# Selective scan: output gate moved into the weights, residual rows added by TensorE, finished tiles copied by ScalarE

## The reference, cut to what matters

```python
shift, scale, gate = split(silu(c) @ ada_w.T + ada_b)    # gate: one row of 512 for each batch
xn = layernorm(x) * (1 + scale) + shift
x_in, z = split(xn @ in_proj_w.T)                        # 1024 channels each
u = silu(causal_conv4(x_in) + conv_b)
dt_r, B, C = split(u @ x_proj_w.T)                       # 64, 16, 16
dt = softplus(dt_r @ dt_proj_w.T + dt_proj_b)
h = h * exp(dt * A) + (dt * u) * B                       # step by step in time, 16 states for each channel
y = (sum over states of h * C) + u * D_param
out = x + gate * ((y * silu(z)) @ out_proj_w.T)
```

## Time and profile before

| | |
|---|---|
| median of 3 runs | 5542.39 us (5534.5 to 5546.62) |
| the profiled execution | 5539.89 us |
| its span | 5538.1 us |
| first stage, first to last instruction of VectorE | to 2130 us of the span |
| busy over the span | TensorE 90%, VectorE 77%, GpSimd 65%, ScalarE 58% |
| mean granted clock of TensorE | 0.97 |

### The profile page before, as it was taken

One profiled execution on the slowest core, in us unless ns is written; L12 is line 12 of the kernel. 1 busy time (PEld: TensorE's weight loads), 2 busy tenths in 40 slices (PEclk: granted clock), 3 DMA queues, 4 the chain that ended last, 5 costly groups with the idle time before them and its releaser, 6 DMA issues. The chain is left out here.

```text
span 5538.1 us, 62588 instructions
## 1 busy us (share of the span) xinstructions
PE 4962.2 (90%) x20224; PEld 2738.9 (49%) x20224; DVE 4265.5 (77%) x5656; ACT 3193.6 (58%) x5887; POOL 3596.6 (65%) x2406
## 2 busy tenths in 40 slices
PE   7888989898989877988999999999998888988998
PEld 2333333333333324764444444444443677776777
DVE  6999999999999995447777777777774565656565
ACT  3757575766667552225888888888886223232323
POOL 3879797978788773224889888988988322222222
PEclk9999999999999998997999999999999999999999
DMA  4021212211121203331111111111111412111212
GB/s 175 23 107 38 92 51 90 89 53 77 53 81 50 91 16 116 133 132 33 28 32 36 24 36 24 36 34 26 36 24 46 157 57 78 37 69 67 78 37 69
DMA packets 119638, 350.72 MB, mean 63 GB/s; under 512 B 13104, under 2 KB 14352, under 8 KB 104912
## 3 DMA queue, kind: packets, MB, share of 16 engines
q1 hardware_dynamic: 102448, 300.76, 16.8%
q0 software_dynamic: 9216, 33.56, 1.6%
q10 hardware_dynamic: 7648, 12.41, 0.7%
HBM read 278.49 MB, written 67.67 MB: 63 GB/s over the span
## 5 line engine op out<-in xcount | busy, mean ns | idle before, releaser
L431 POOL TENSOR_TENSOR mamba_hc<-mamba_h,mamba_bc 128x1024 f32<-128x1024 f32 x512 | 1217.0, 2377 | 353.6 <-DVE mamba_h L664 299.7
L812 PE MATMUL mamba_y<-mamba_hc,ident 128*128 128x512 f32 x2048 | 1004.7, 614 | 262.9 <-POOL mamba_hc L431 261.8
L1364 POOL TENSOR_TENSOR attn_pair_sum<-attn_pair_sum,attn_prob 128x1024 f32<-128x1024 f32 x512 | 1203.9, 2386 | 54.0 <-ACT attn_prob L1479 54.0
L1523 DVE TENSOR_REDUCE attn_mx<-attn_ps_max 128x1 f32<-128x512 f32 x1536 | 967.7, 685 | 317.2 <-PE attn_ps_max L1387 312.7
L1479 ACT ACTIVATE attn_prob<-attn_ps_s 128x512 f32<-128x512 f32 x2048 | 1051.3, 602 | 76.4 <-PE attn_ps_s L1414 76.4
L534 ACT ACTIVATE mamba_da<-mamba_dt,mamba_a_neg 128x512 f32<-128x512 f32 x1024 | 690.0, 689 | 692.7 <-DVE mamba_h L664 689.4
L664 DVE TENSOR_TENSOR_SCAN mamba_h<-mamba_da,mamba_state,mamba_h 128x512 f32<-128x512 f32 x768 | 940.1, 1266 | 1.9 <-ACT mamba_da L534 1.9
L1414 PE MATMUL attn_ps_s<-attn_q_stack,attn_k_stack 100*128 100x512 f32 x2048 | 884.9, 436 | 5.2 <-ACT attn_prob L1479 5.2
L1387 PE MATMUL attn_ps_max<-attn_k_stack,attn_q_stack 98*128 98x512 f32 x2048 | 833.2, 412 | 37.7 <-DMA attn_q_stack<-qk_parts 19.8
L812 PEld LDWEIGHTS mamba_y<-mamba_hc,ident 128*128 128x128 f32 x2048 | 371.4, 192 | 844.1 <-POOL mamba_hc L431 429.5
L654 DVE TENSOR_TENSOR mamba_h<-mamba_du,mamba_bc 128x1024 f32<-128x1024 f32 x512 | 619.6, 1210 | 65.5 <-POOL mamba_state L433 57.3
(11 more groups left out here) (302 smaller groups left out, 7475.1 us busy)
## 6 DMA issues: line engine op xcount, KB each, us to landing
mamba_bc<-bc_dram SPq DMA_DIRECT2D x64, 1024.0 KB, 7.3
mamba_w<-in_in_proj_w_T SPq DMA_DIRECT2D x16, 2048.0 KB, 7.8
qk_parts<-qkv_pair POOLq DMA_DIRECT2D x64, 512.0 KB, 3.2
attn_k_stack<-qk_parts SPq DMA_DIRECT2D x96, 256.0 KB
attn_q_stack<-qk_parts SPq DMA_DIRECT2D x96, 256.0 KB
mamba_x_in<-in_x SPq DMA_DIRECT2D x16, 1024.0 KB, 5.6
mamba_w<-in_out_proj_w_T SPq DMA_DIRECT2D x8, 2048.0 KB, 8.4
lin_norm_x<-x_after_L SPq DMA_DIRECT2D x16, 1024.0 KB, 5.6
```

What stands on the lines that cost most here:

```text
L431: nc.gpsimd.tensor_tensor(hc[:, gs % HC_SLOTS, :, :], h[:, gs % H_SLOTS, :, :], bc[:, g, G:2 * G, :], ALU.mult).then_inc(s["hc_done"], 1)
L812: mm = nc.tensor.matmul(y[ct % 2][:, :], ident[:, :], hc[:, gs % HC_SLOTS, j, :], start=(g == 0 and j == 0), stop=(g == NG - 1 and j == G ...
L1364: nc.gpsimd.tensor_tensor(pair_sum[(hd * NGRP + g) % 2][:, at], first[:, at], prob[unit % SLOTS][:, at], ALU.add).then_inc(s["sum_done"], 1)
L1523: nc.vector.tensor_reduce(to, ps_max[seq % BANKS][:, :], AX.X, ALU.max, negate=own_block(i)).then_inc(s["bank_read"], 1)
```

## The change

It does three things.

1. `gate_out`: GpSimd multiplies the output weights of each chunk by the gate, in place, one slice of 128x512 for each of the eight channel tiles, in the steps of the new table `GATE_W` (36, 41, 44, 49, 52, 55, 56, 57). The first slice waits for the weights' load; TensorE waits for the slices that it uses.
2. `project_back`: after the eighth channel tile TensorE adds the residual rows with one more matmul, identity times `x_in`, 512 columns wide: four for each chunk.
3. `take_out`: ScalarE copies the finished tile out of PSUM into `x_in`, in the same steps of `OUT_READ`, after the two decays of the step. VectorE's `add_residual` is gone, and with it lines 679 and 682.

```diff
+        GATE_W = {36: 0, 41: 1, 44: 2, 49: 3, 52: 4, 55: 5, 56: 6, 57: 7}
@@ gpsimd
+            def gate_out(it, k):
+
+                if k == 0:
+                    q = turn_of["out", it]
+                    pool.wait_ge(w_in[q % 2], (q // 2 + 1) * 16)
+                    if it % NC_B == 0:
+                        wait_freed(pool, "cg", 0, it // NC_B)
+                w = w_view("out", it)[:, k, :]
+                nc.gpsimd.tensor_tensor(w, w, gate[:, it // NC_B, :], ALU.mult).then_inc(s["w_gated"], 1)
...
                     if i in GATE:
                         gate_y(it, GATE[i])
+                    if i in GATE_W:
+                        gate_out(it, GATE_W[i])
@@ scalar
+            def take_out(it, t):
+
+                bank = wait_full(act, "out", it, t)
+                nc.scalar.activation(x_in[:, t, :], bank[:, :], ACT.Copy).then_inc(freed("out", it, t), 1)
...
                         softplus(it, ct + 1)
+                    if it and i in OUT_READ:
+                        take_out(it - 1, OUT_READ.index(i))
...
+            for t in range(TT):
+                take_out(NCH - 1, t)
@@ vector
-            def add_residual(it, t):
-
-                if it == 0 and t == 0:
-                    wait_freed(dve, "cg", 0, NB - 1)
-                bank = wait_full(dve, "out", it, t)
-                nc.vector.tensor_tensor(bank[:, :], bank[:, :], gate[:, it // NC_B, :], ALU.mult).then_inc(s["out_gated"], 1)
-                dve.wait_ge(s["out_gated"], it * TT + t + 1)
-                dve.wait_ge(s["residual_in"], (it + 1) * 16)
-                nc.vector.tensor_tensor(x_in[:, t, :], bank[:, :], x_in[:, t, :], ALU.add).then_inc(freed("out", it, t), 1)
...
-                    if it and i in OUT_READ:
-                        add_residual(it - 1, OUT_READ.index(i))
...
-            for t in range(TT):
-                add_residual(NCH - 1, t)
@@ tensor
             def project_back(it, t, part):
-                if t == 0 and part == 0:
-                    wait_weights("out", it)
+                if t == 0:
+                    pe.wait_ge(s["w_gated"], it * CT + 2 * part + 2)
                 pe.wait_ge(s["gated"], it * CT + 2 * part + 2)
                 if part == 0:
                     begin("out", it, t)
                 for k in range(2 * part, 2 * part + 2):
                     mm = nc.tensor.matmul(at("out", it, t)[:, :], zy[:, k, t * P:(t + 1) * P], w_view("out", it)[:, k, :],
-                                          start=(k == 0), stop=(k == CT - 1))
+                                          start=(k == 0), stop=False)
                 if part == 3:
+                    pe.wait_ge(s["residual_in"], (it + 1) * 16)
+                    mm = nc.tensor.matmul(at("out", it, t)[:, :], ident[:, :], x_in[:, t, :], start=False, stop=True)
                     mm.then_inc(s["work_full"], 1)
```

More of the change, by code:

```diff
@@ L271, in stage_mamba @@
                  "drive_done exp_done scan_done state_saved hc_done sum_done y_read gated z_done tap_done tap_added u_done "
-                 "xp_read bc_written out_gated residual_in stored own_act own_norm setup_done zero_done "
+                 "xp_read bc_written w_gated residual_in stored own_act own_norm setup_done zero_done "
                  "u_begun gate_b_in cond_in small_in gate_w_in silu_done ident_done neg_done sum_set")
```

## The result

The changed kernel takes 5557.73 us (median of 20 runs, 5547.01 to 5566.6) against 5543.79 us before (median of 20 runs, 5534.5 to 5561.98). The ratio is 1.0024, with a 95% interval of 1.0016 to 1.0031: slower by 13 us, with 9 to 17 us in the interval. The forecast was +11.4 us and 5553.8 us. The profiled execution has a span of 5553.0 us against 5538.1.

What follows compares the result with a forecast made beforehand. VectorE was taken to bound each chunk's early steps and GpSimd steps 36 to 55 of chunks 0 to 6. Terms -36.7 - 0.5 + 41.4 + 2.8 + 1.7 + 2.7 = +11.4 us gave 5553.8 us, range 5538 to 5568.

Steps and rivals of the forecast that it cites:

- The bound that changes owner: In each chunk VectorE bounds steps 0 to 37; GpSimd bounds steps 36 to 55 of chunks 0 to 6.
- VectorE's gain: Steps 7, 8, 12, 16 of chunks 1 to 7: 28 removed pairs save 36.7 us, a vanished wait 0.5 us.
- GpSimd's five multiplications before hc 55 and the port: Chunks 0 to 6: multiplications cost 5.9 us a chunk, 41.4 us; port conflicts at steps 40, 48, 56 add 2.8 us.
- The last chunk: Chunk 7, steps 40, 48 and 56: line 647 waits 0.56 us each for a later GpSimd instruction, +1.7 us.
- The tail: After the last scan: four identity matmuls add 3.5 us, ScalarE's shorter copy gives back 0.8 us, net +2.7 us.
- TensorE and ScalarE inside the loop: Identities cost 3.4 us a chunk against 7.4 us of stall and slow matmuls given up; ScalarE's copies charged nothing.
- the room of 3.8 us: TensorE's slack before GpSimd's step 16, from the matmul after sums 13 at 903.7 us to hc 16 at 907.50.
- The rival in which the stall stays and the identities come on top: TensorE becomes the bound of steps 5 to 28, 4.8 us short in seven chunks: +45 us, 5588; chance 0.07.
- The sum: All terms added: -36.7 - 0.5 + 41.4 + 2.8 + 1.7 + 2.7 = +11.4 us, giving 5553.8.

Runs made afterwards that it cites:

- e1: The changed kernel without the gate multiplications on GpSimd, so the gate is left out of the computation: 5510.81 us, ratio 0.9936 to the kernel before.
- e2: The changed kernel with the same eight multiplications on GpSimd at steps 32, 33, 56 to 59 and the next chunk's 0 and 1: 5527.90 us, ratio 0.9959.
- e5: The changed kernel with the multiplications of steps 36, 44 and 52 put two steps later (38, 46, 54): 5554.19 us, one execution.
- e3: The changed kernel with the eight multiplications on VectorE, after its scans of steps 37 to 53, instead of GpSimd: 5552.01 us, ratio 1.0006 to the kernel before.
- e6: The changed kernel without the four identity matmuls a chunk, so the residual is left out of the computation: 5545.6 us, one execution.
- e4: The changed kernel with the four finished tiles copied by VectorE in place of ScalarE: 5574.05 us, ratio 1.0051 to the kernel before.

## Why the prediction was right

**The bound that changes owner.** Right. The earlier trace rows and the empty list of GpSimd's waits said it, e1 and e2 show it: the multiplications cost 45.5 us of the chunks in the steps of the change and 8.3 us in steps with room.

**VectorE's gain**, forecast 36.7 + 0.5 = 37.2 us. Measured to drive 18 in chunks 1 to 7: 37.9 us. The pairs are as forecast, 5.31 us for four in a chunk. The rest, in chunks 2 to 4, is 0.7 us and not 0.5, because with the wait at drive 16 the longer line 647 of the earlier trace rows (0.89 us) goes too.

**GpSimd's five multiplications before hc 55 and the port**, forecast 5.9 + 0.4 = 6.3 us a chunk, 44.2 us. Measured 6.28 to 6.39 us, 44.4 us together. GpSimd's order in chunk 3, hc against hc, gives the parts. The five arrive with 1.22, 1.08, 1.19, 1.09 and 1.21 us, 5.8 together. The three meetings with line 669 cost 0.19, -0.03 and +0.19 us more than those with line 647 did, 0.35 together where 0.4 was forecast. The remaining 0.2 us come behind the multiplication of step 55, where I had 0.06: in chunk 0 drive 58 has become 6.10 us later, drive 59 6.26 and drive 60 6.29. e5 is shorter by 0.6 us a chunk, and not by these 0.35, since its own meeting at drive 48 came out 0.2 us cheaper than in the kernel before. The shape was as forecast: line 669 at 1.70 us where I had said 1.8 to 2.0, then 0.66 us for the saved column, and the mean of line 404 down by the 44 ns that the tap additions had lost. VectorE's own share of a meeting is hidden in chunks 0 to 6, as drive 40 above shows, and not in chunk 7: +1.85 us after the change, 0.0 in e5.

The Trainium skill's page "SBUF — State Buffer", section "SBUF: two separate sides", says that of a VectorE instruction with two SBUF inputs and a GpSimd instruction that reads SBUF the one that starts first has the shared port pair for its whole length and the other waits. e3 shows it at its plainest: 2.84 us for an instruction of 0.67 that started 0.42 us after a GpSimd instruction of 2.70. These runs agree. Where the two start level, the recorded starts do not tell which is first: in chunk 3 of the kernel before line 647 started 0.02 us ahead of the tap addition at drive 40 and still took 1.84 us, and 0.04 us ahead at drive 48, where it took 0.67.

**The last chunk** +1.7, measured +1.85. **The tail** +2.7, measured 2.5 to the last tile (35.31 less 32.77; the 2.6 above is a difference of rounded numbers); e6 puts the identities at 3.5, as forecast, so ScalarE's shorter copy gives back 0.9, forecast 0.8.

**TensorE and ScalarE inside the loop** at nothing: right for both (e1, e6). TensorE was forecast 4.0 us earlier by step 24; its first z matmul came 2.9 to 4.6 us earlier, 4.45 in chunk 3. But the room of 3.8 us was measured at the wrong place, at the sums that hc 16 needs. e4 shows that TensorE reaches VectorE sooner, by the softplus of step 12, where the kernel before had no room at all in chunks 2 to 4. That changes no term of the sum, because the change made TensorE earlier. The rival in which the stall stays and the identities come on top could not happen in that form, as e4 shows: two of them fill part of the stall.

**The sum** was 11.4 us. The stage's own difference without the 1.2 us before chunk 0 is 8.4 + 2.6 = 11.0 us, so the agreement is term by term and not only in the total. The measured 13 us have an interval of 9 to 17 and cannot tell the two apart. One execution of each could not have shown the sign: the length of the later stages, 3393 to 3412 us over the nine profiles, varies by more than the effect. That their part of the difference was small, 2.2 us in the two profiles, was not forecast.

## What to carry to other kernels

Moving work off the busiest engine pays only at the steps where that engine is the bound, and the engine that takes it must have room at its own steps; look for both in stretches, not in the shares of the page, and then choose the steps (here 37 us lay in a table of eight numbers). Where an engine's list of waits is empty over a stretch and the others wait for it, expect every operation added there to arrive in full, as the five did here. The room of an engine that runs late is to be measured at every place where another waits for what it makes, and the nearest one counts. When the effect is smaller than the spread of whole runs, compare the starts of one repeated instruction in two traces: in most chunks they agreed to 0.1 us where whole times differed by 10.

## What the hardware showed

In these traces an instruction of VectorE with two SBUF inputs that starts behind a running GpSimd instruction ends only after that one has ended, and its recorded time includes the wait: 0.67 us alone, between 0.7 and 1.9 us where it met one, and 2.84 us once. GpSimd's instruction pays when it is the second: 0.66 us for one of 0.19, 2.70 us for one of 2.35. The wait is not listed as a wait; it appears as a longer instruction. The later stages, unchanged in all runs, took between 3393.3 us (e6) and 3412.0 us (e2) from the first statistics of the second stage to the end; what sets this was not looked into.
